# A recommender forward pass on one core: the last twenty of 80 indirect gathers issued back to back

## The chip, the cores and the metric

One NeuronCore of a Trainium2 chip runs the kernel; the other cores are idle. The metric is the device time in microseconds of one execution, and for several executions their median. The profiler records one execution; its "span" is the time from the first to the last instruction that it shows.

## The reference

A wide-and-deep model scores 2048 samples. Each sample has 13 dense numbers and eight category indices.

```python
wide = dense @ Wd_wide
for si, wi in zip(S, w):                 # eight tables of one weight per row
    wide = wide + wi[si]
wide = wide + wc0[S[3] * VOCABS[4] + S[4]]   # 140,625 rows
wide = wide + wc1[S[5] * VOCABS[6] + S[6]]   # 500,000 rows
deep_in = jnp.concatenate([dense @ Wd_deep] + [Ei[si] for Ei, si in zip(E, S)], axis=1)
h = jax.nn.relu(deep_in @ W1)            # 576 -> 512
h = jax.nn.relu(h @ W2)                  # 512 -> 256
return bias + h @ W3 + wide
```

All is float32. VOCABS is [125000, 25000, 12500, 375, 375, 1000, 500, 100], and each embedding row has 64 numbers.

## The kernel before

The 2048 samples are 16 tiles of 128, in four blocks of 512. Fields 0 to 2 have large tables, and their rows (64 embedding numbers and the wide weight, 65 in all) are fetched from HBM by indirect DMAs. The five small fields are looked up by matmuls: VectorE writes a one-hot matrix (`build_onehot`, L463) and TensorE multiplies it with the table (`look_up`, L634; `look_up_wide`, L646). The two crossed terms, `wc0` and `wc1`, are one float per sample out of large tables, and are fetched by indirect DMAs into `cross`. TensorE does layers 1 and 2 as three float32r products each (`product`, L663 to L665); ScalarE and VectorE split values into a high and a low part (L339, L343, L483, L488).

Every engine has its program written out in order, and semaphores join them.

GpSimd (POOL) issues all 80 indirect DMAs, one per tile and field, each for 128 rows. Their order is: for each of the four blocks eight gathers into `x_pair` (L289) and four into `x_two` (L297), which makes 48; then 32 gathers into `cross` (L307), c = 0 for 16 tiles and c = 1 for 16 tiles. In block 0 the 12 gathers follow one another with nothing between them. From block 1 on each gather is followed by a "pause": a memset of 128 x 320 float32 into `pause_sb`, a buffer that nobody reads (L282). Before each memset but the first, POOL waits until the one before has counted up the semaphore `paused` (L281); the memsets are all on POOL, so that wait is over when it comes. Only the very last gather, number 31 of `cross`, has no pause behind it. This document numbers the gathers of `cross` 0 to 31, as `c * TILES + t`. There are 67 pauses: 36 in blocks 1 to 3, and 31 among those of `cross`.

Each gather counts a semaphore up by 16 when its data has landed: `rows_gathered` per block for the rows, `cross_gathered[0]` and `cross_gathered[1]` for the two halves of `cross`.

The end of the kernel is on VectorE, in program order (L590 to L606): the wide sums of the gathered rows (L593, L594, L596); after a wait for all 16 gathers of c = 0 the sum with `cross[:, 0, :]` and the bias (L599); `weigh_first` and `weigh_second` of the last block (L497, L508), which TensorE's `layer3` (L720) multiplies out; the sum with the deep part (L604); and after a wait for all 16 gathers of c = 1 the last sum (L606). SyncE then stores `result` (L263).

Of the kernel before, what the change touches and what calls it, by code (L numbers as in the profile page):

```python
# [20 lines left out]
NX = len(CROSSES)  # L21
SPLIT = 3

TILES = BATCH // P
# [21 lines left out]
IDX_ROWS = NL * TILES  # L46
WARM_UP = 8
BUSY = [4, 5]


IO_ORDER = [("spread", 0, i) for i in range(NL)] + [("look", 0, i) for i in range(4)]
# [21 lines left out]
def program(nc, index, dense_t, big, small, small_w, wc, wd_rep_t, wd_wide, w1, w2, w3, bias, out):  # L73
# [6 lines left out]
    with ExitStack() as ctx:  # L80
# [185 lines left out]
        @block.gpsimd  # L266
        def _(pool):
            nc.gpsimd.memset(zero[:], 0.0).then_inc(zero_ready, 1)
            nc.gpsimd.iota(row_id[:], pattern=[[P, max(CHUNKS)]], base=0, channel_multiplier=1,
                           allow_small_or_imprecise_dtypes=True).then_inc(row_id_ready, 1)  # L270
            pool.wait_ge(zero_ready, 1)
            for m in (ident16, ident):
                nc.gpsimd.affine_select(out=m[:], in_=zero[:], compare_op=ALU.not_equal, fill=1.0, base=0,
                                        pattern=[[-1, P]], channel_multiplier=1).then_inc(ident_ready, 1)
            pool.wait_ge(ident_ready, 2)
            nc.gpsimd.memset(look_w_parts[:], 0.0).then_inc(look_w_zeroed, 1)
            nc.gpsimd.memset(ones[:], 1.0).then_inc(ones_ready, 1)
            def pause(n):

                if n:  # L280
                    pool.wait_ge(paused, n)  # L281
                nc.gpsimd.memset(pause_sb[:], 0.0).then_inc(paused, 1)  # L282

            pool.wait_ge(gather_index_ready, 1)
            pauses = 0
            for b in range(BLOCKS):
                for t in range(b * BT, (b + 1) * BT):
                    for g in (0, 1):
                        nc.gpsimd.indirect_dma_start(  # L289
                            out=x_pair[:, t, g * ROW:(g + 1) * ROW], out_offset=None, in_=big[g],  # L290
                            in_offset=bass.IndirectOffsetOnAxis(ap=idx_gather[:, g, t:t + 1], axis=0),
                        ).then_inc(rows_gathered[b][0], 16)
                        if b > 0:
                            pause(pauses)
                            pauses += 1
                for t in range(b * BT, (b + 1) * BT):
                    nc.gpsimd.indirect_dma_start(  # L297
                        out=x_two[:, t, :], out_offset=None, in_=big[2],
                        in_offset=bass.IndirectOffsetOnAxis(ap=idx_gather[:, 2, t:t + 1], axis=0),
                    ).then_inc(rows_gathered[b][1], 16)  # L300
                    if b > 0:
                        pause(pauses)
                        pauses += 1
            pool.wait_ge(cross_index_ready, 1)
            for c in range(NX):
                for t in range(TILES):
                    nc.gpsimd.indirect_dma_start(  # L307
                        out=cross[:, c, t:t + 1], out_offset=None, in_=wc[c],
                        in_offset=bass.IndirectOffsetOnAxis(ap=idx_cross[:, c, t:t + 1], axis=0),
                    ).then_inc(cross_gathered[c], 16)  # L310
                    if (c, t) != (NX - 1, TILES - 1):
                        pause(pauses)
                        pauses += 1

# [294 lines left out]
        def _(pe):  # L609
# [17 lines left out]
            def look_up(b, i):  # L627
                use = ("look", b, i)
                io_free(use)
                if b == 0 and i in (0, 2, 4):  # L630
                    pe.wait_ge(table_low, 1 + i // 2)
                for c in range(CHUNK0[i], CHUNK0[i] + CHUNKS[i]):
                    pe.wait_ge(onehot_ready, b * NCH + c + 1)
                    last = nc.tensor.matmul(io_bank(use)[:], table_hl[:, c, :], onehot[:, c, :],  # L634
                                            start=c == CHUNK0[i], stop=c == CHUNK0[i] + CHUNKS[i] - 1)
                last.then_inc(io_full, 1)
# [87 lines left out]
            def keep_busy(n):  # L724

                for _ in range(n):
                    nc.tensor.matmul(l1_ps[M1 - 1][:], zero16[:, 0:P], zero16[:], start=True, stop=True)
# [12 lines left out]
            look_up(0, 1)  # L740
            keep_busy(BUSY[0])
            pe.wait_ge(wd_loaded, 32)
            pe.wait_ge(row_index_ready, 1)
            nc.tensor.matmul(l2_ps[0:NROWS, :], wd_rep[:], w1d_sb[:], start=True, stop=True).then_inc(wdense_done, 1)
            keep_busy(BUSY[1])
            look_up(0, 2)
# [95 lines left out]
```

## Time and profile before

| | us |
|---|---|
| median of 3 runs | 136.67 |
| lowest and highest | 136.29 and 137.22 |
| the profiled execution, its own time | 137.18 |
| its span | 135.3 |

The profiled execution spent 137.18 - 135.3 = 1.9 us outside of its span. Busy time is the time in which an engine executed instructions; DMA-issuing instructions of SyncE and ScalarE are not counted as busy, but POOL's indirect DMAs are, since GpSimd works on each of them. "issue" is idle time for which the profile shows no releaser. In rows of a timeline the columns are start, duration, engine, line, operation, and in brackets how long the engine was idle before it.

### The profile page before, as it was taken

How to read it: one execution, taken by the hardware profiler on the slowest of the kernel's cores; microseconds unless marked ns; L12 is line 12 of the kernel's file. 1: busy time of each engine (PE TensorE's matmuls, PEld its weight loads, DVE VectorE, ACT ScalarE, POOL GpSimd, SP SyncE). 2: the span in 40 equal slices, each digit the busy share in tenths (PEclk: the TensorE clock that was granted, in tenths of full speed). 3: DMA queues.
4: the chain of work that ended last, by engine and by line, in shares of the span. 5: the costliest groups of instructions: out<-in, count | busy, mean ns of one | idle time of the engine just before them, and what ended most of it. 6: DMA issues, size and time to landing. Idle time of an engine off the chain costs nothing.

```text
span 135.3 us, 1728 instructions
## 1 busy us (share of the span) xinstructions
PE 112.7 (83%) x588; PEld 83.4 (62%) x588; DVE 71.7 (53%) x163; ACT 55.0 (41%) x97; POOL 110.9 (82%) x157
## 2 busy tenths in 40 slices
PE   6979999929779999999999999999999999920000
PEld 2544875726566886687888858878886788920000
DVE  2696984822399905868980166999304019310000
ACT  3698946131925224248261515456242325210000
POOL 5587877999899999989999989999998998989800
PEclk9999999995999999999999999999999999995555
DMA  4958436868632232223323320000000000000000
GB/s 138 306 115 277 29 66 28 218 122 224 207 27 22 20 26 22 20 20 20 25 19 26 22 20 0 0 0 0 5 0 0 1 0 0 5 0 0 0 3 0
DMA packets 6096, 6.90 MB, mean 51 GB/s; under 512 B 2931, under 2 KB 4115, under 8 KB 6088
## 3 DMA queue, kind: packets, MB, share of 16 engines
q0 software_dynamic: 2560, 1.62, 15.8%
q1 hardware_dynamic: 3096, 4.45, 10.8%
q10 hardware_dynamic: 432, 0.72, 1.5%
q8 instruction: 5, 0.08, 0.2%
q14 instruction: 3, 0.02, 0.1%
HBM read 6.60 MB, written 0.19 MB: 50 GB/s over the span
## 4 chain that ended last, share of the span: by engine, by line
POOL 79%; issue 11%; DMA 4%; DVE 1%; POOLq 1%; DVEq 0%
POOL x_pair L289 25%; POOL cross L307 21%; POOL pause_sb L282 21%; POOL x_two L297 12%; DMA idx_raw<-in_index_dram 2%; DMA cross<-in_wc_dram,idx_cross 2%; POOLq L80 1%; DVE idx_wrap L443 0%; DVE idx_sum L445 0%; DVE idx_look L448 0%; DVE result L606 0%; DVE idx_gather L448 0%; DVEq L605 0%
## 5 line engine op out<-in xcount | busy, mean ns | idle before, releaser
L463 DVE TENSOR_SCALAR onehot<-idx_bc,row_id 128x512 fp32r<-128x512 f16 x76 | 39.5, 586 | 4.7 <-PE io_ps L646 1.9
L289 POOL DMA_INDIRECT x_pair<-in_rows_dram,idx_gather x32 | 33.3, 1041 | 8.5 <-issue 6.2
L307 POOL DMA_INDIRECT cross<-in_wc_dram,idx_cross x32 | 30.9, 965 | 5.3 <-issue 5.3
L282 POOL MEMSET pause_sb<- 128x320 f32 x67 | 29.0, 434 | 0.0
L663 PE MATMUL l_ps<-xt_hi,w_hi 128*128 128x512 f32 x64 | 25.6, 400 | 0.0
L665 PE MATMUL l_ps<-xt_hi,w_lo 128*128 128x512 f32 x64 | 25.1, 392 | 0.0
L664 PE MATMUL l_ps<-xt_lo,w_hi 128*128 128x512 f32 x64 | 25.0, 391 | 0.0
L634 PE MATMUL io_ps<-onehot,table_hl 128*128 128x512 f32 x76 | 21.9, 414 | 0.2
L483 DVE TENSOR_TENSOR xt_lo<-io_ps,xt_hi 128x512 fp32r<-128x512 f32 (+1 forms) x8 | 5.5, 687 | 28.4 <-ACT xt_hi L339 27.5
L326 ACT CAST xt_hi<-io_ps 64x512 fp32r<-64x512 f32 x20 | 11.6, 579 | 19.8 <-PE io_ps L634 18.9
L297 POOL DMA_INDIRECT x_two<-in_rows_dram,idx_gather x16 | 16.1, 1004 | 3.2 <-issue 3.2
L634 PEld LDWEIGHTS io_ps<-onehot,table_hl 128*128 128x128 f32 x76 | 14.4, 193 | 4.4 <-DVE onehot L463 0.7
L663 PE MATMUL l_ps<-h_hi,w_hi 128*128 128x512 f32 (+1 forms) x36 | 13.4, 373 | 1.6 <-DVE h_lo L488 1.6
L352 ACT ACTIVATE h<-l_ps 128x512 f32<-128x512 f32 (+1 forms) x9 | 5.0, 551 | 22.2 <-PE l_ps L665 22.2
L663 PEld LDWEIGHTS l_ps<-xt_hi,w_hi 128*128 128x128 f32 x64 | 12.0, 188 | 2.8 <-issue 0.5
L665 PEld LDWEIGHTS l_ps<-xt_hi,w_lo 128*128 128x128 f32 x64 | 12.0, 188 | 2.6
L664 PEld LDWEIGHTS l_ps<-xt_lo,w_hi 128*128 128x128 f32 x64 | 12.0, 188 | 2.4
L665 PE MATMUL l_ps<-h_hi,w_lo 128*128 128x512 f32 (+1 forms) x36 | 13.3, 368 | 0.0
L664 PE MATMUL l_ps<-h_lo,w_hi 128*128 128x512 f32 (+1 forms) x36 | 13.2, 366 | 0.0
L488 DVE SCALAR_TENSOR_TENSOR h_lo<-l_ps,h_hi 128x512 fp32r<-128x512 f32 x16 | 10.2, 685 | 3.8 <-ACT h_hi L343 3.8
L327 ACT CAST xt_lo<-io_ps 64x512 fp32r<-64x512 f32 x20 | 11.7, 583 | 0.5
L343 ACT ACTIVATE h_hi<-l_ps 128x512 fp32r<-128x512 f32 x16 | 8.7, 600 | 3.2 <-PE l_ps L665 2.8
(75 smaller groups left out, 106.8 us busy)
## 6 DMA issues: line engine op xcount, KB each, us to landing
idx_bc<-idx_dram SPq DMA_DIRECT2D x3, 640.0 KB, 4.9
w_sb<-in_w_dram ACTq DMA_DIRECT2D x2, 256.0 KB
x_pair<-in_rows_dram,idx_gather POOLq DMA_INDIRECT x32
w_sb<-in_w_dram SPq DMA_DIRECT2D x2, 256.0 KB
w_sb<-in_w_dram SPq DMA_DIRECT2D x1, 512.0 KB
cross<-in_wc_dram,idx_cross POOLq DMA_INDIRECT x32
dense_stack<-dense_dram SPq DMA_DIRECT2D x3, 156.0 KB
table<-in_small_dram SPq DMA_DIRECT2D x1, 416.0 KB
```

Source lines behind the costliest of these rows:

```text
L282: nc.gpsimd.memset(pause_sb[:], 0.0).then_inc(paused, 1)
L289: nc.gpsimd.indirect_dma_start(out=x_pair[:, t, g * ROW:(g + 1) * ROW], out_offset=None, in_=big[g], in_offset=bass.IndirectOffsetOnAxis(a ...
L297: nc.gpsimd.indirect_dma_start(out=x_two[:, t, :], out_offset=None, in_=big[2], in_offset=bass.IndirectOffsetOnAxis(ap=idx_gather[:, 2, t: ...
L307: nc.gpsimd.indirect_dma_start(out=cross[:, c, t:t + 1], out_offset=None, in_=wc[c], in_offset=bass.IndirectOffsetOnAxis(ap=idx_cross[:, c ...
L326: nc.scalar.copy(xt_hi[b % 2][to, g, :], bank[0:D, :]).then_inc(io_act, 1)
L327: nc.scalar.copy(xt_lo[b % 2][to, g, :], bank[D:2 * D, :]).then_inc(io_act, 1)
L463: nc.vector.tensor_scalar(onehot[:, CHUNK0[i] + c, :], idx_bc[:, b, i, :], row_id[:, c:c + 1], None, ALU.is_equal).then_inc(onehot_ready, 1)
L488: nc.vector.scalar_tensor_tensor(out=h1_lo[:, m, :], in0=l1_ps[m][:], scalar=0.0, in1=h1_hi[:, m, :].bitcast(f32), op0=ALU.max, op1=ALU.su ...
L634: last = nc.tensor.matmul(io_bank(use)[:], table_hl[:, c, :], onehot[:, c, :], start=c == CHUNK0[i], stop=c == CHUNK0[i] + CHUNKS[i] - 1)
L663: nc.tensor.matmul(dst, w_hi, a_hi, start=start, stop=False)
L664: nc.tensor.matmul(dst, w_hi, a_lo, start=False, stop=False)
L665: return nc.tensor.matmul(dst, w_lo, a_hi, start=False, stop=stop)
```

## The change

A constant `DENSE_END = 20` is added, and the condition under which a gather of `cross` is followed by a pause is changed. Before, every one but number 31 was; now only numbers 0 to 11 are (32 - 20 = 12). The pauses behind numbers 12 to 30, 19 of them, are gone. The count `pauses` goes on as before, so POOL's waits for `paused` still match the memsets that remain.

```diff
 WARM_UP = 8
 BUSY = [4, 5]
+
+DENSE_END = 20
...
                         in_offset=bass.IndirectOffsetOnAxis(ap=idx_cross[:, c, t:t + 1], axis=0),
                     ).then_inc(cross_gathered[c], 16)
-                    if (c, t) != (NX - 1, TILES - 1):
+                    if c * TILES + t < NX * TILES - DENSE_END:
                         pause(pauses)
                         pauses += 1
```

## Rows read from the trace of the kernel before

**Rows 1.** The page: busy time by engine, then the chain that ended last.

```profile
PE 112.7 (83%) x588; PEld 83.4 (62%) x588; DVE 71.7 (53%) x163; ACT 55.0 (41%) x97; POOL 110.9 (82%) x157
...
POOL 79%; issue 11%; DMA 4%; DVE 1%; POOLq 1%; DVEq 0%
```

**Rows 2.** The last steps of the chain, in time: start, duration, what.

```profile
127.50 2.34 DMA cross<-in_wc_dram,idx_cross
...
129.93 0.17 DVE result L606
```

**Rows 3.** Waits of the whole run: the last sum of VectorE.

```profile
DVE result L606 <- DMA cross<-in_wc_dram,idx_cross: 9.7, 1, 9.7
```

**Rows 4.** Timeline of POOL: the gathers of cross from number 12 on.

```profile
98.69 0.95 POOL L307 DMA_INDIRECT cross<-in_wc_dram,idx_cross  x1 [0.16 <-issue]
99.65 0.38 POOL L282 MEMSET pause_sb<- 128x320 f32 x1
100.19 0.95 POOL L307 DMA_INDIRECT cross<-in_wc_dram,idx_cross  x1 [0.17 <-issue]
...
103.18 0.95 POOL L307 DMA_INDIRECT cross<-in_wc_dram,idx_cross  x1 [0.16 <-issue]
...
116.64 1.35 POOL L307 DMA_INDIRECT cross<-in_wc_dram,idx_cross  x1 [0.17 <-issue]
...
127.50 0.95 POOL L307 DMA_INDIRECT cross<-in_wc_dram,idx_cross  x1 [0.17 <-issue]
```

**Rows 5.** Timeline of POOL: gathers without pauses, block 0 and the first of block 1.

```profile
4.59 1.27 POOL L289 DMA_INDIRECT x_pair<-in_rows_dram,idx_gather  x1 [2.26 <-DVE idx_gather L448]
...
12.43 0.94 POOL L289 DMA_INDIRECT x_pair<-in_rows_dram,idx_gather  x1 [0.30 <-issue]
13.68 1.31 POOL L289 DMA_INDIRECT x_pair<-in_rows_dram,idx_gather  x1 [0.30 <-issue]
15.30 1.88 POOL L289 DMA_INDIRECT x_pair<-in_rows_dram,idx_gather  x1 [0.30 <-issue]
...
20.37 0.94 POOL L297 DMA_INDIRECT x_two<-in_rows_dram,idx_gather  x1 [0.30 <-issue]
...
23.33 0.94 POOL L289 DMA_INDIRECT x_pair<-in_rows_dram,idx_gather  x1 [0.30 <-issue]
```

**Rows 6.** Timeline of VectorE beside those gathers.

```profile
12.60 0.69 DVE L469 TENSOR_TENSOR w_lo<-w_sb,w_hi 128x512 fp32r<-128x512 f32 x1 [1.28 <-ACT w_hi L360]
...
15.39 1.67 DVE L463 TENSOR_SCALAR onehot<-idx_bc,row_id 128x512 fp32r<-128x512 f16 x4
...
20.86 0.69 DVE L483 TENSOR_TENSOR xt_lo<-io_ps,xt_hi 128x512 fp32r<-128x512 f32 x1 [0.95 <-issue]
```

**Rows 7.** Windows: each engine's busy us (x instructions), PEclk, DMA share, GB/s.

```profile
4.59:23.33 18.74, 17.52 (x100) 11.46 (x98) 14.32 (x34) 14.58 (x28) 15.08 (x12) 1.00 0.58 121
...
98.69:127.50 28.81, 20.71 (x128) 16.69 (x126) 7.40 (x15) 7.27 (x13) 25.66 (x38) 0.90 0.02 1
```

**Rows 8.** Timeline of VectorE from 98.69 us on.

```profile
102.51 0.69 DVE L483 TENSOR_TENSOR xt_lo<-io_ps,xt_hi 128x512 fp32r<-128x512 f32 x1 [6.68 <-ACT xt_hi L339]
103.12 0.79 DVE L508 SCALAR_TENSOR_TENSOR h_w<-h,w_sb,h_first 128x512 f32<-128x512 f32 x1
108.04 0.68 DVE L483 TENSOR_TENSOR xt_lo<-io_ps,xt_hi 64x512 fp32r<-64x512 f32 x1 [4.13 <-ACT xt_hi L339]
111.48 2.73 DVE L488 SCALAR_TENSOR_TENSOR h_lo<-l_ps,h_hi 128x512 fp32r<-128x512 f32 x4 [2.76 <-ACT h_hi L343]
...
114.78 0.23 DVE L599 SCALAR_TENSOR_TENSOR wide_bias<-cross,bias_sb,wide_dense 128x16 f32<-128x16 f32 x1
116.41 0.75 DVE L497 SCALAR_TENSOR_TENSOR h_first<-h,w_sb,wide_look 128x512 f32<-128x512 f32 x1 [1.40 <-issue]
117.62 0.48 DVE L508 SCALAR_TENSOR_TENSOR h_w<-h,w_sb,h_first 128x256 f32<-128x256 f32 x1 [0.46 <-ACT h L352]
118.91 0.48 DVE L508 SCALAR_TENSOR_TENSOR h_w<-h,w_sb,h_first 128x256 f32<-128x256 f32 x1 [0.80 <-ACT h L352]
120.09 0.17 DVE L604 TENSOR_TENSOR wide_deep<-wide_bias,deep_ps 128x16 f32<-128x16 f32 x1 [0.70 <-PE deep_ps L720]
```

**Rows 9.** The page: DMA issues, kind, count and median us to landing.

```profile
x_two<-in_rows_dram,idx_gather POOLq DMA_INDIRECT x16, 3.3
```

## The prediction

> **What bounds the kernel now.** I read the page's busy line first, and it alone would mislead: TensorE is busy 83% of the span and POOL 82% [rows 1]. The chain that ended last decides between them: 79% of it is POOL, 11% is POOL's own issue time, and TensorE is not in it at all [rows 1]. The end of that chain says why. The last gather of `cross` starts at 127.50 us and has landed 2.34 us later; VectorE's last sum starts at 129.93 us, and what follows it to the end of the span (135.3 - 129.93 = 5.4 us: the sum, the store and the closing of the program) hangs on nothing else [rows 2]. The waits confirm it from the other side: before that sum VectorE was idle for 9.7 us, until the gather had landed [rows 3]. So the deep part of the model had been ready for a long time: VectorE had added it in by 120.09 + 0.17 = 120.26 us [rows 8]. The kernel is a single file of 80 gathers on POOL, and whatever shortens the file by up to some 9 us shortens the kernel by as much.
>
> The timeline of POOL gives the pace of the file. With a pause one step takes 0.95 us of gather, 0.38 us of memset and 0.17 us of issue, 1.50 us in all [rows 4]. Without one (block 0) the best steps are 0.94 us of gather and 0.30 us of issue: from 12.43 to 13.68 is 1.25 us [rows 5].
>
> **What the change removes.** The pauses behind gathers 12 to 30 go, 19 of them; number 31 had none. Gather 12 still starts at 98.69 us, since all that lies before it is untouched. From there to the start of gather 31 at 127.50 us are 28.81 us for 19 steps [rows 4], 1.516 us each: 1.50 us, and once 0.40 us more, at 116.64 us, where a gather took 1.35 us.
>
> **What a step costs afterwards.** The memset's 0.38 us goes, but not all of it is won. Between a memset and the next gather POOL shows 0.17 us of issue, between two gathers 0.30 us [rows 4, 5]. So 0.13 us comes back, and a step is 0.94 + 0.30 = 1.245 us (between 1.24 and 1.25 by the rows). 19 x 1.245 = 23.66 us, if no gather is stretched. Bounds for the issue gap: it may be 0.17 us as after a memset, which would make a step 1.12 us, or 0.30 us as between two gathers. I take 0.30 us, since it is measured between exactly such a pair of instructions, eleven times in block 0 and once before the first of block 1.
>
> **Stretched gathers.** In block 0 not all steps were 1.245 us: from 4.59 to 23.33 us 12 steps took 18.74 us, 1.562 us each [rows 5, 7]. That is slower than with pauses, and it is what speaks against this change. The excess is 18.74 - 12 x 1.245 = 3.80 us. The gathers that were long lay beside VectorE's work: the one of 1.88 us at 15.30 us ran beside four one-hots that lasted 1.67 us [rows 5, 6]. VectorE was busy 14.32 us of that stretch [rows 7]. In the stretch of the change it is busy 7.40 us of 28.81 [rows 7], so I carry over a rate and not a number. Two of its kinds of work there, L483 and L488 (0.69 + 0.68 + 2.73 = 4.1 us), read one operand from PSUM and one from SBUF [rows 8]; the only one of that kind in block 0, at 20.86 us, lay beside a gather of the plain 0.94 us, the one at 20.37 us [rows 5, 6]. Without that kind the rate is 3.80 / (14.32 - 0.69) = 0.28 us of stretch for each us of VectorE, and the dense stretch has 7.40 - 4.1 = 3.3 us of it: 0.92 us. Ends: 0 us (as at 12.60 us, where a subtraction with both operands in SBUF lay inside a gather of 0.94 us, and at 103.12 us, where L508 lay beside a gather of 0.95 us) [rows 4, 5, 6, 8]; and 7.40 x 3.80 / 14.32 = 1.96 us if every kind counts. I take 0.9 us.
>
> The sum, against the profiled execution's own time: 28.81 - 23.66 - 0.9 = 4.25 us less. Gather 31 starts at 98.69 + 24.56 = 123.25 us, has landed at 125.6 us, the span ends at 135.3 - 4.25 = 131.05 us, and that execution would have taken 137.18 - 4.25 = 132.9 us. The profiled execution is 0.5 us above the median of the runs, 136.67; the saving doesn't hang on that, so the median goes to 136.67 - 4.25 = 132.4 us.
>
> **What is late next, and what hides it.** The deep part is complete at 120.26 us, 5.3 us ahead of the last landing in the forecast; it does not take over. If the issue gap were 0.17 us and nothing was stretched, the last landing would be at 98.69 + 19 x 1.12 + 2.34 = 122.3 us, still behind it. Denser gathers may also slow VectorE's work in the tail; that would have to cost over 5 us of delay before it counted. The wait for `cross_gathered[0]` ahead of L599 does not matter: gather 15 started at 103.18 us before the change [rows 4], so it had landed near 105.5 us, and VectorE came to L599 only at 114.78 us [rows 8]. The time from a gather's start to its landing could grow with more of them in flight. The rows give 2.34 us in the quiet end [rows 2] and a median of 3.3 us for gathers into `x_two` [rows 9], with rows of 260 bytes and mostly beside other transfers. DMA is 2% busy in the stretch of the change and 58% in block 0 [rows 7], so I take 2.34 us, and keep 1 us more as an end.
>
> A rule speaks against the gain. By the Trainium skill, page "SBUF — State Buffer", section "Who interferes with whom", a VectorE instruction with two SBUF inputs contends with a GpSimd instruction that reads SBUF, and whoever comes second is blocked until the other has finished. The same section infers that such an instruction leaves descriptor generation alone, since it holds only the read interface. By the first reading the sum would be that of the third rival below, by the second the saving would be the full 5.15 us. The rows lie between them: nothing at 12.60 us, something beside the one-hots.
>
> **The rivals.**
>
> *Block 0's pace returns (slightly slower).* If the stretching is not VectorE's doing but comes with gathers that follow one another, a step is 1.562 us: 19 x 1.562 = 29.68 us, 0.87 us more than now, 137.5 us. For it: the pace was measured over 12 steps. Against it: 20.37 us and 23.33 us show plain gathers of 0.94 us inside the same unbroken run, and DMA traffic and VectorE were both far busier there. Chance 0.03.
>
> *The gathers back up (slower).* POOL may only be so many gathers ahead of the landing; once that room is used up, each gather waits for a landing, and a step becomes 2.34 us. The 12 gathers of block 0 and the first of block 1 went without such a wait, so it decides from the thirteenth gather of an unbroken run on. The new run has 20, so 8 steps are longer by 2.34 - 1.245 = 1.1 us each, 8.8 us, against 4.25 us saved: 4.5 us more, 141.2 us. For it: no unbroken run of that length is in the trace. Against it: at a step of 1.25 us and 2.34 us to landing only two are in flight at a time. Chance 0.02.
>
> *VectorE shuts POOL out (less gain).* Each instruction of VectorE with both large operands in SBUF holds up the gather beside it for its whole length: 0.79 + 0.75 + 0.48 + 0.48 = 2.50 us [rows 8]. Then 28.81 - 23.66 - 2.50 = 2.65 us are saved, 134.0 us. For it: the gather at 116.64 us, beside L497 at 116.41 us, was 0.40 us longer [rows 4, 8]. Against it: that is half of L497's length, and at 103.12 us nothing was lost. Chance 0.12.
>
> *The issue gap shrinks to 0.17 us (more gain).* 28.81 - 19 x 1.12 - 0.9 = 6.6 us, 130.0 us. For it: the stretch has idle engines all around. Against it: 0.30 us came out the same in each of the twelve cases. Chance 0.03.
>
> That the change does nothing has little room: the memsets are on POOL's own chain and the chain is the end. Something that I have not seen gets 0.01 of no change.
>
> **How the numbers follow.** My forecast, 132.4 us, gets 0.79; its own spread comes from the stretch (0 to 1.96 us: 131.5 to 133.5 us) and from the landing (up to 1 us more). The range takes in the rival at 134.0 us as its upper end, and goes below 131.5 us by 0.3 us for the scatter of the medians: 131.2 to 134.0 us. A difference of about 1%, 1.4 us, is what a measurement of this kernel can tell from none. Faster by more: the forecast, the shut-out and the shrunken gap, 0.79 + 0.12 + 0.03 = 0.94. Within it: block 0's pace and the unseen, 0.04. Slower: the backing up, 0.02.
>
> **What would show it.** In the changed kernel's timeline of POOL, 48 memsets of `pause_sb` instead of 67; gather 12 of `cross` near 98.7 us; between the gathers behind it 0.30 us of issue and no memset; most of them 0.94 to 0.95 us long, and a few longer ones, all beside VectorE's L497 and L508. VectorE's wait ahead of L606 should be 9.7 - 4.25 = 5.4 us and still end with the gather. The prediction is wrong if the gathers beside L488 are stretched, if the gap is not 0.30 us, if gathers from the thirteenth on take longer than those before, if the last one takes much more than 2.34 us to land, or if L604 ends later than 125 us.

## The result, and the profile after

The changed kernel took 145.22 us (median of 4 runs, 143.91 to 145.59) beside 136.84 us before: a ratio of 1.060, with an interval of 1.052 to 1.068. It is slower by 8.4 us where 132.4 us was forecast. The profiled execution took 143.91 us, its span is 142.1 us.

The page of the changed kernel (its line numbers are 2 higher), busy time and the chain that ended last:

```profile
PE 121.0 (85%) x588; PEld 86.7 (61%) x588; DVE 71.6 (50%) x163; ACT 54.9 (39%) x97; POOL 102.1 (72%) x138
...
PE 69%; another core or an unknown queue 13%; issue 7%; ACT 5%; DVE 2%; ACTq 1%; DVEq 0%
```

Against [rows 1] POOL is gone from the chain and TensorE is in it. But POOL did exactly what was forecast. Its timeline, the last pause, the gathers 12 to 14 and the last:

```profile
96.04 0.55 POOL L284 MEMSET pause_sb<- 128x320 f32 x1
96.75 1.03 POOL L309 DMA_INDIRECT cross<-in_wc_dram,idx_cross  x1 [0.16 <-issue]
98.09 1.19 POOL L309 DMA_INDIRECT cross<-in_wc_dram,idx_cross  x1 [0.30 <-issue]
99.58 0.94 POOL L309 DMA_INDIRECT cross<-in_wc_dram,idx_cross  x1 [0.30 <-issue]
...
121.31 0.94 POOL L309 DMA_INDIRECT cross<-in_wc_dram,idx_cross  x1 [0.30 <-issue]
```

From gather 12 to gather 31 are 121.31 - 96.75 = 24.56 us, the number of the forecast to the digit (in part by luck, see below); before it was 28.81 us [rows 4]. Gather 12 started 1.9 us earlier than before, since the twelve dense gathers of block 0 went faster in this execution. POOL was done at 122.25 us. The time was lost elsewhere. The waits of the changed kernel:

```profile
DVE xt_lo L485 <- ACT xt_hi L341: 40.2, 7, 18.7
ACT wide_look L336 <- remote: 24.2, 2, 19.0
...
DVE onehot L465 <- remote: 6.4, 1, 6.4
```

"remote" (on the page "another core or an unknown queue") stands for a wait whose release the trace does not hold. Only one core runs here, so it isn't another core. The longest such wait is ScalarE's, for the copy of the last block's wide look-up. The timelines of TensorE and of ScalarE around it:

```profile
107.61 1.32 PE L648 MATMUL io_ps<-onehot,look_w_parts 128*32 128x512 bf16 x19
...
111.83 0.27 PE L661 MATMUL io_ps<-ident,x_two 128*65 128x128 f32 x1 [0.34 <-issue]
...
116.81 0.58 PE L665 MATMUL l_ps<-xt_hi,w_hi 128*128 128x512 f32 x1 [0.86 <-issue]
...
122.47 0.59 PE L667 MATMUL l_ps<-xt_hi,w_lo 128*128 128x512 f32 x1 [1.52 <-issue]
127.14 0.80 PE L665 MATMUL l_ps<-xt_hi,w_hi 128*128 128x512 f32 x1 [4.08 <-DVE xt_lo L485]
```

```profile
105.73 0.59 ACT L341 CAST xt_hi<-io_ps 128x512 fp32r<-128x512 f32 x1
125.31 0.59 ACT L336 COPY wide_look<-io_ps 128x512 f32<-128x512 f32 x1 [18.98 <-remote]
125.79 0.58 ACT L341 CAST xt_hi<-io_ps 64x512 fp32r<-64x512 f32 x1
```

TensorE finished the 19 matmuls at 107.61 + 1.32 = 108.93 us. A signal is here the semaphore update by which TensorE tells other engines that a matmul is done. The copy waits for that of the last of the 19, and for `h2_used` of block 1, which is long past. It starts at 125.31 us: the signal came 16.4 us late. The transposes of `x_two` end at 112.10 us, and their copy starts right behind the first one, so both signals were there once the gathers had ended. In between TensorE itself hardly moves: from 112.53 to 122.47 us it starts 12 matmuls that need nothing but TensorE's own queue, many of them 0.7 to 2.1 us apart.

The rest is passed on. VectorE's L485 of that block starts at 126.40 us where it started at 108.04 us before [rows 8], 18.4 us later. The idle time then costs 1.4 us more. Its sequel, from there to L606, takes 139.88 - 126.40 = 13.5 us instead of 12.05 us, with the granted clock at 1.2 GHz for the first twelve matmuls behind the gap (0.50 of full speed from 118 to 132.4 us), 0.43 us apart instead of 0.23 us. So the last sum waits for the deep part now: L606 (L604 before) starts at 139.88 us. The last sum starts at 140.09 us, 10.2 us later than before, and the close behind it takes 2.0 us, not 5.4 us (more on that at the end): 10.2 - 3.4 = 6.8 us, the difference of the spans. Some 4 us of the 18.4 us were lost earlier, in block 0, whose twelve gathers always were dense: there ScalarE's first wide copy came at 28.19 us, for matmuls that had ended at 22.99 us; in the trace of the kernel before it came at 24.03 us.

### The profile page after: what moved, and what is told of

The parts are those of the page before. It is cut to its first block, busy times and chain, and to the rows that moved or that the text cites. A ratio compares the mean times of both kernels' runs of the same rounds, so it can differ in the third digit from the quotient of the medians.

```text
span 142.1 us, 1709 instructions
## 1 busy us (share of the span) xinstructions
PE 121.0 (85%) x588; PEld 86.7 (61%) x588; DVE 71.6 (50%) x163; ACT 54.9 (39%) x97; POOL 102.1 (72%) x138
## 3 DMA queue, kind: packets, MB, share of 16 engines
q0 software_dynamic: 2560, 1.62, 16.3%
## 4 chain that ended last, share of the span: by engine, by line
PE 69%; another core or an unknown queue 13%; issue 7%; ACT 5%; DVE 2%; ACTq 1%; DVEq 0%
PE l_ps L665 16%; PE l_ps L667 15%; PE l_ps L666 15%; PE io_ps L636 12%; PE io_ps L648 3%; PE io_ps L661 2%; PE l_ps L695 2%; PE l_ps L729 1%; DVE onehot L465 1%; PE deep_ps L722 1%; ACT idx_bc L321 1%; ACT L358 1%; ACT xt_hi L341 1%; PE l_ps L746 1%
## 5 line engine op out<-in xcount | busy, mean ns | idle before, releaser
L291 POOL DMA_INDIRECT x_pair<-in_rows_dram,idx_gather x32 | 32.0, 1000 | 8.4 <-issue 6.2
L665 PE MATMUL l_ps<-xt_hi,w_hi 128*128 128x512 f32 x64 | 27.4, 428 | 5.7 <-DVE xt_lo L485 4.1
L667 PE MATMUL l_ps<-xt_hi,w_lo 128*128 128x512 f32 x64 | 26.7, 418 | 3.0 <-issue 2.9
L666 PE MATMUL l_ps<-xt_lo,w_hi 128*128 128x512 f32 x64 | 26.5, 414 | 0.3 <-issue 0.3
L485 DVE TENSOR_TENSOR xt_lo<-io_ps,xt_hi 128x512 fp32r<-128x512 f32 (+1 forms) x8 | 5.5, 687 | 41.8 <-ACT xt_hi L341 40.2
L284 POOL MEMSET pause_sb<- 128x320 f32 x48 | 21.4, 445 | 0.0
L665 PEld LDWEIGHTS l_ps<-xt_hi,w_hi 128*128 128x128 f32 x64 | 12.8, 199 | 11.1 <-DVE xt_lo L485 5.1
L665 PE MATMUL l_ps<-h_hi,w_hi 128*128 128x512 f32 (+1 forms) x36 | 14.2, 394 | 3.2 <-issue 3.2
L667 PEld LDWEIGHTS l_ps<-xt_hi,w_lo 128*128 128x128 f32 x64 | 12.8, 200 | 6.0 <-issue 3.3
L666 PEld LDWEIGHTS l_ps<-xt_lo,w_hi 128*128 128x128 f32 x64 | 12.9, 201 | 4.4 <-issue 2.0
L336 ACT COPY wide_look<-io_ps 128x512 f32<-128x512 f32 x4 | 2.3, 586 | 30.2 <-remote 24.2
L490 DVE SCALAR_TENSOR_TENSOR h_lo<-l_ps,h_hi 128x512 fp32r<-128x512 f32 x16 | 10.2, 684 | 5.1 <-ACT h_hi L345 5.1
```

Of the source, the lines that this page charges most:

```text
L291: nc.gpsimd.indirect_dma_start(out=x_pair[:, t, g * ROW:(g + 1) * ROW], out_offset=None, in_=big[g], in_offset=bass.IndirectOffsetOnAxis(a ...
L490: nc.vector.scalar_tensor_tensor(out=h1_lo[:, m, :], in0=l1_ps[m][:], scalar=0.0, in1=h1_hi[:, m, :].bitcast(f32), op0=ALU.max, op1=ALU.su ...
L665: nc.tensor.matmul(dst, w_hi, a_hi, start=start, stop=False)
L666: nc.tensor.matmul(dst, w_hi, a_lo, start=False, stop=False)
L667: return nc.tensor.matmul(dst, w_lo, a_hi, start=False, stop=stop)
```

## The experiments

The versions ran in six groups, each group within minutes on one chip, beside runs of the kernel before. Of the edits only the lines that matter are shown. Some versions leave work out: the short look-up 15 of the 19 table chunks of the last block, the version without gathers the last twenty gathers, the versions with half the rows 64 rows of each of them. Where gathers or rows are left out, `cross` is zeroed beforehand. Theory A was that TensorE's signals are held up when its burst of short matmuls (the wide look-up) falls into the dense run. Theory B was the length or pace of the dense run, whatever TensorE does. Theory C was a condition of the chip or of the time, which the dense gathers only let show.

**1 to 4 (first group): where the dense run stands, the burst, a break, no gathers.**

```diff
-DENSE_END = 20
+DENSE_END = 12
```

> Only the last twelve gathers follow one another without a pause; the run then starts near 110 us, when TensorE has its wide look-up of the last block (19 short matmuls) behind it. Theory A (TensorE's semaphore updates are held back only if its burst of short matmuls falls into the dense run): no stall, 11 pauses less at 0.25 us each, 136.8 - 2.8 = 134 us. Theory B (it is the length of the dense run: after some ten gathers at a step of 1.25 us something is full, whatever TensorE does): a stall only from about 122 us on, when the deep part is done, so also about 134 us, or slower if it comes sooner. Theory C (any dense run beside TensorE's full stream holds it back): over 137 us.

```diff
-                for c in range(NCH):
+                for c in (range(NCH) if b < BLOCKS - 1 else range(groups)):
...
-                                            start=c < groups, stop=c >= NCH - groups)
+                                            start=c < groups, stop=c >= (NCH if b < BLOCKS - 1 else groups) - groups)
```

> The changed kernel with its twenty dense gathers; the wide look-up of the last block is cut from 19 matmuls to 4 (15 of its 19 table chunks are left out). Theory A: without the burst no stall, the gathers decide and the time is 132 to 133 us. Theory B: ScalarE still waits long for its copy of the wide look-up or for the value after it, 140 us and more.

```diff
+                    elif c * TILES + t < NX * TILES - 1:
+                        pause(pauses, 1)
+                        pauses += 1
```

> The changed kernel, but each of the last gathers is again followed by a memset, of one column in place of 320 (about 0.10 us): the step is 0.95 + 0.10 + 0.17 = 1.22 us, as without a pause. If the pace of the gathers does it, the stall is there and the time 142 to 146 us. If a break by another instruction is enough, whatever its length, there is no stall and the time is near 131 to 132 us.

```diff
+                    if c * TILES + t >= NX * TILES - DENSE_END:
+                        for _ in range(2):
+                            pool.wait_ge(paused, pauses)
+                            nc.gpsimd.memset(pause_sb[:].bitcast(bf16), 0.0).then_inc(paused, 1)
+                            pauses += 1
+                        continue
...
-            dve.wait_ge(cross_gathered[1], 16 * TILES)
+            dve.wait_ge(paused, 36 + NX * TILES - DENSE_END + 2 * DENSE_END)
```

> The last twenty gathers are left out (that part of the crossed terms is zero) and POOL is kept busy by two memsets of 0.63 us in the place of each, a step of about 1.27 us. If gathers are what holds TensorE back, no stall: POOL ends near 98.7 + 20 x 1.27 = 124 us and the deep part at 120 to 124 us, total about 130 to 132 us. If the stall has nothing to do with the gathers' own work, it stays.

Measured beside 137.69 us of the kernel before: 134.70 us with twelve dense gathers (ratio 0.978, 0.973 to 0.982), and in one run each 132.2 us with the short look-up, 131.93 us with the narrow memsets and 134.95 us without gathers. The last is above the 130 to 132 us expected because the two memsets took 1.38 us and not 1.27 us. No trace of the four has a "remote" wait. It looked like theory A, and like a break being enough. Neither follows, because the changed kernel had not been run in that group.

**5 and 6 (second group): the changed kernel again, and the narrow memset timed.**

> The changed kernel itself, unaltered, on a chip beside runs of the kernel before. The runs with a narrow memset and with a short look-up had no stall, but neither has been compared with the changed kernel on one chip. If the dense run and the burst do it, the changed kernel is at 143 to 146 us here too, with ScalarE waiting some 19 us for its copy of the wide look-up. Theory C (the stall belongs to a condition of the chip or of the recording under which the first comparison ran, and the dense gathers only let it show): no stall here, 132 to 133 us, about 0.965 of before.

> The twenty last gathers, each followed by a memset of one column, timed beside the changed kernel: 131.9 us again. Theory A and the theory of the pace leave it without a stall only if the break itself matters; theory C has it equal to the changed kernel within 0.5%.

The changed kernel took 144.07 us beside 137.92 us (1.048, 1.040 to 1.056). The narrow memset, 131.93 us in the first group, took 138.14, 144.05, 144.57 and 144.28 us here. In three of four runs a break in the run didn't help, and the group matters. The trace is of the run of 138.14 us. TensorE's last matmul of layer 1, then ScalarE's four copies, one for each bank of layer 1:

```profile
110.79 0.39 PE L670 MATMUL l_ps<-xt_hi,w_lo 128*128 128x512 f32 x1
```

```profile
113.28 0.60 ACT L348 ACTIVATE h_hi<-l_ps 128x512 fp32r<-128x512 f32 x1 [5.89 <-remote]
116.14 0.60 ACT L348 ACTIVATE h_hi<-l_ps 128x512 fp32r<-128x512 f32 x1 [2.25 <-remote]
121.07 0.60 ACT L348 ACTIVATE h_hi<-l_ps 128x512 fp32r<-128x512 f32 x1 [4.33 <-remote]
125.33 0.60 ACT L348 ACTIVATE h_hi<-l_ps 128x512 fp32r<-128x512 f32 x1 [3.67 <-remote]
```

All four banks were done by 111.18 us. Their signals came one at a time, all before the last gather of the dense run ended (124.49 + 0.95 = 125.44 us). So the signals are not shut out for the length of the run; they get through slowly.

From then on a version is only read beside a sign of which condition its group was in.

**7 to 10 (third group): the changed kernel, and three of the four versions beside it.**

> The changed kernel beside the three that follow, all on one chip, since the narrow memset took 131.9 us on one chip and 138 to 144 us on another, and the changed kernel was never on the first. If the stall depends on the chip, this reads either 132 to 133 us or 143 to 146 us; the others are to be read against it.

> The wide look-up of the last block cut from 19 matmuls to 4 (15 of 19 table chunks left out). Beside a changed kernel that stalls: under theory A 132 to 133 us; if the pace of the gathers alone does it, beside any full stream of TensorE, 140 us and more. Beside one that doesn't stall: no information.

> The last twenty gathers left out, memsets of 2 x 0.63 us in the place of each. Beside a changed kernel that stalls: if gathers load what TensorE's signals need, 134.9 us and no stall; if it is anything about POOL being busy, a stall and 140 us and more.

> The last twelve gathers dense. Beside a changed kernel that stalls: theory A gives 134 to 135 us with no wait of ScalarE over 4 us; if a dense run anywhere in TensorE's last 10 us of work is enough, TensorE ends later than 120 us and the time is over 137 us.

Beside 136.66 us: the changed kernel 143.63 us (1.049, 1.029 to 1.068), the short look-up 134.48 and 138.43 us, no gathers 134.42 us, twelve dense gathers 134.34 us (0.981, 0.967 to 0.995).

The trace of the changed kernel shows whose signals are late. ScalarE:

```profile
103.20 0.58 ACT L336 COPY wide_look<-io_ps 128x512 f32<-128x512 f32 x1 [3.49 <-PE io_ps L648]
111.03 0.58 ACT L341 CAST xt_hi<-io_ps 64x512 fp32r<-64x512 f32 x1 [7.25 <-remote]
127.17 2.06 ACT L345 ACTIVATE h_hi<-l_ps 128x512 fp32r<-128x512 f32 x4 [15.56 <-remote]
```

TensorE, VectorE and POOL of the same trace:

```profile
104.02 0.60 PE L661 MATMUL io_ps<-ident,x_two 128*65 128x128 f32 x4
...
112.38 0.80 PE L665 MATMUL l_ps<-xt_hi,w_hi 128*128 128x512 f32 x1 [5.01 <-issue]
...
117.24 0.45 PE L667 MATMUL l_ps<-xt_hi,w_lo 128*128 128x512 f32 x1
```

```profile
111.64 0.68 DVE L485 TENSOR_TENSOR xt_lo<-io_ps,xt_hi 64x512 fp32r<-64x512 f32 x1 [10.55 <-issue]
127.80 2.48 DVE L490 SCALAR_TENSOR_TENSOR h_lo<-l_ps,h_hi 128x512 fp32r<-128x512 f32 x4 [15.48 <-ACT h_hi L345]
```

```profile
122.66 0.94 POOL L309 DMA_INDIRECT cross<-in_wc_dram,idx_cross  x1 [0.30 <-issue]
```

ScalarE's copy ends at 111.61 us and VectorE starts at 111.64; VectorE ends at 112.32 and TensorE starts at 112.38. Those signals take 0.03 and 0.06 us. TensorE's own are late: the transposes end at 104.62 us and ScalarE starts 6.4 us later; the first bank of layer 1 is done 3 matmuls behind 112.38 us, at 114.03 us, and ScalarE starts at 127.17 us, 13 us later and 3.6 us after the last gather's end. The lateness grows along the dense run and ends some 3 us behind its last gather. TensorE meanwhile does its 12 matmuls at their usual spacing for 1.2 GHz (0.43 us) and then has nothing left that it may do.

The short look-up refutes theory A as it was put. Without the burst the signals were late as well, only later:

```profile
106.98 2.64 ACT L345 ACTIVATE h_hi<-l_ps 128x512 fp32r<-128x512 f32 x4 [2.86 <-PE l_ps L667]
116.23 0.60 ACT L354 ACTIVATE h<-l_ps 128x512 f32<-128x512 f32 x1 [6.61 <-remote]
127.48 0.66 ACT L354 ACTIVATE h<-l_ps 128x256 f32<-128x256 f32 x2 [10.66 <-remote]
```

By 110 us TensorE's signals were still in time, and the four copies of layer 1 were through. The last two signals of layer 2, for matmuls that ended near 113 and 114.6 us, came together at 127.48 us. The burst may still add to the lateness: with it the first late signal was that of the transposes that ended at 104.62 us. How much it adds was not measured.

Without gathers at the end nothing was late there, in the same group. Its only "remote" waits lie in block 0, where the gathers stayed dense:

```profile
DVE onehot L474 <- remote: 4.6, 1, 4.6
...
ACT wide_look L345 <- remote: 2.2, 1, 2.2
```

So at the end it is the gathers, and not POOL being busy; which part of a gather does it (its descriptors, its transfers or its sixteen semaphore updates) no version separates. With twelve dense gathers the signals were late too, but the deep part had 5 us in hand, and it ended at 121.45 us, ahead of the last landing:

```profile
117.73 0.38 ACT L354 ACTIVATE h<-l_ps 128x256 f32<-128x256 f32 x1 [3.28 <-remote]
```

```profile
121.28 0.17 DVE L606 TENSOR_TENSOR wide_deep<-wide_bias,deep_ps 128x16 f32<-128x16 f32 x1 [2.65 <-remote]
```

**11 to 14 (fourth group): the control, two paces, half the rows.** The pause of 160 columns is the edit of the narrow memset with 160 in place of 1.

> The changed kernel as the control of its chip for the three that follow: 143 to 146 us, with waits of ScalarE of 14 us and more for a signal of TensorE, if this chip is like three of the four seen so far.

> Each of the last nineteen steps has a memset of 160 columns (about 0.22 us): the step is 0.95 + 0.22 + 0.17 = 1.34 us, halfway between 1.25 and 1.50. If TensorE's signals fall behind in proportion to how far the pace is above what is bearable, the delay is smaller than the changed kernel's by about half: 137 to 141 us. If there is a sharp bound between 1.34 and 1.50 us per step it is 142 to 146 us; if it is between 1.25 and 1.34 us, no stall and 136.8 - 19 x 0.16 = 134 us.

```diff
+                    rows = P if c * TILES + t < NX * TILES - DENSE_END else P // 2
-                        out=cross[:, c, t:t + 1], out_offset=None, in_=wc[c],
+                        out=cross[0:rows, c, t:t + 1], out_offset=None, in_=wc[c],
...
-                    if c * TILES + t < NX * TILES - DENSE_END:
+                    if c * TILES + t < NX * TILES - 1:
                         pause(pauses)
```

> The last twenty gathers fetch 64 rows in place of 128 (the other half of these crossed terms is left at zero), and each is followed by the full memset. If GpSimd's time of a gather is mostly per row, a step is about 1.1 us, so that more gathers but fewer rows come in a microsecond than in the changed kernel. If the rows (descriptors and their packets) are what the signals of TensorE queue behind: no stall, and 136.8 - 19 x 0.4 = 129 us. If it is the number of gathers, each with its sixteen semaphore updates: a stall and over 138 us.

```diff
-DENSE_END = 20
+DENSE_END = 12
...
-                nc.gpsimd.memset(pause_sb[:], 0.0).then_inc(paused, 1)
+                nc.gpsimd.memset(pause_sb[:, 0:240], 0.0).then_inc(paused, 1)
```

> A version that may beat both: the last twelve gathers dense as before, and all other pauses 240 columns long (0.30 us in place of 0.38), a step of 1.42 us. 56 pauses save 0.08 us each, 4.5 us, on top of 2.8: 129.5 us if the signals of TensorE stay in time, and POOL's last gather lands near 119 us, about with the deep part. If 1.42 us is already too fast, TensorE falls behind over the whole second half and the time is over 137 us.

Beside 137.05 us the unaltered changed kernel took 132.90 and 132.97 us: a ratio of 0.969 (0.961 to 0.976). That is the forecast, and not the 143 to 146 us expected by then. Its timelines of POOL and of VectorE:

```profile
99.07 0.95 POOL L309 DMA_INDIRECT cross<-in_wc_dram,idx_cross  x1 [0.17 <-issue]
100.33 1.37 POOL L309 DMA_INDIRECT cross<-in_wc_dram,idx_cross  x1 [0.30 <-issue]
102.00 0.94 POOL L309 DMA_INDIRECT cross<-in_wc_dram,idx_cross  x1 [0.30 <-issue]
...
123.23 0.94 POOL L309 DMA_INDIRECT cross<-in_wc_dram,idx_cross  x1 [0.30 <-issue]
```

```profile
117.10 0.17 DVE L606 TENSOR_TENSOR wide_deep<-wide_bias,deep_ps 128x16 f32<-128x16 f32 x1 [0.70 <-PE deep_ps L722]
125.81 0.17 DVE L608 TENSOR_TENSOR result<-wide_deep,cross 128x16 f32<-128x16 f32 x1 [8.54 <-DMA cross<-in_wc_dram,idx_cross]
```

The nineteen steps take 24.16 us, one gather is stretched by 0.43 us, the last sum waits for the gather for 8.5 us, and no wait is "remote". The same program is worth -4 us or +6 to +8 us, by a condition that the kernel does not set. The other three say little about the late signals in such a group: 133.30 and 135.54 us with 160 columns, 137.20 us with half the rows and full pauses, 132.13 us with pauses of 240 columns (0.963, 0.957 to 0.969; 129.5 us was expected). Half the rows did not make a gather much shorter, 0.90 to 0.91 us instead of 0.95, so that expectation of a step of 1.1 us failed (it was 1.45 us), and the time was that of the kernel before.

**15 to 18 (fifth and sixth group): the two open questions, once without and once with late signals.** In half_dense the last twenty gathers have 64 rows and no pauses.

> All pauses but the last 240 columns long, the last twelve gathers dense: 132.1 us on a chip on which the changed kernel had no stall. On a chip of the other kind, where TensorE's signals come late in a dense run: if 1.42 us a step is borne, again 132 to 133 us, with a delay only in the last twelve steps; if not, lateness grows over blocks 1 to 3 and the time is over 137 us.

> The last twenty gathers without pauses and with 64 rows each in place of 128 (the other half of these crossed terms is left at zero): a step of about 0.91 + 0.30 = 1.21 us, so as many gathers and as many semaphore updates as in the changed kernel, and half the rows. On a chip of the kind with late signals: 144 us if the number of gathers does it, 132 to 133 us if their rows do. On the other kind of chip 132 us, and no information.

> As the two runs before, once more, since both fell on chips without late signals: 132 us there. On a chip with late signals 132 to 133 us if 1.42 us a step is borne, over 137 us if not.

> As before, once more, for the other kind of chip: 144 us if the number of gathers loads TensorE's signals, 132 to 133 us if their rows do; 132 us and no information on a chip without late signals.

In the fifth group both took 132 us (132.09 and 132.32 beside 137.40). The sixth came on the same chip, number 10, and there half the rows took 144.27 and 144.15 us beside 137.25 us (1.052, 1.046 to 1.058), and the pauses of 240 columns took 144.74, 145.48, 132.27 and 136.80 us. ScalarE and POOL in the trace with half the rows:

```profile
102.95 0.59 ACT L345 CAST xt_hi<-io_ps 128x512 fp32r<-128x512 f32 x1
122.49 0.58 ACT L340 COPY wide_look<-io_ps 128x512 f32<-128x512 f32 x1 [18.95 <-issue]
126.83 0.58 ACT L345 CAST xt_hi<-io_ps 64x512 fp32r<-64x512 f32 x1 [3.75 <-remote]
```

```profile
120.45 0.90 POOL L313 DMA_INDIRECT cross<-in_wc_dram,idx_cross  x1 [0.30 <-issue]
121.65 0.90 POOL L313 DMA_INDIRECT cross<-in_wc_dram,idx_cross  x1 [0.31 <-issue]
```

Two things follow. The condition isn't a trait of the chip, since chip 10 had both. And halving the rows doesn't help, since 20 gathers of 64 rows hold TensorE's signals for as long as 20 of 128: the wide copy starts 16.3 us behind its matmuls, which ended at 106.15 us (16.4 us in the first trace). From 128 to 64 rows the lateness goes with the number of gathers in a time, and not with the rows. Theories B and C both hold in part: the dense gathers are needed, and so is a condition that changes with time.

Whether a step of 1.42 us is already too fast is not decided. That version has twelve dense gathers at the end as well, and twelve in block 0 like every version. Its trace (the run of 144.74 us) has late signals long behind block 0's dense run, whose last gather ends at 25.11 us. TensorE's second look-up for block 1 and ScalarE's copy of it:

```profile
35.30 0.96 PE L636 MATMUL io_ps<-onehot,table_hl 128*128 128x512 f32 x3 [2.50 <-issue]
```

```profile
41.97 0.58 ACT L328 CAST xt_hi<-io_ps 64x512 fp32r<-64x512 f32 x1 [6.11 <-remote]
```

But so has the first trace of the changed kernel, in the same place, with full pauses and a step of 1.50 us:

```profile
33.45 0.97 PE L636 MATMUL io_ps<-onehot,table_hl 128*128 128x512 f32 x3
```

```profile
36.41 0.58 ACT L328 CAST xt_hi<-io_ps 64x512 fp32r<-64x512 f32 x1 [2.72 <-remote]
```

The signal is 5.7 us late with the short pauses and 2.0 us late with the full ones. ScalarE's four wide copies, one per block, start 3.72, 1.03, 0.05 and 4.86 us behind the end of their matmuls with the short pauses, and 5.20, 0.73, 0.05 and 16.38 us with the full ones. So behind block 0 the lateness dies away at either step. But with the short pauses TensorE has lost more by then: L510 of block 2 starts at 113.60 us, in the fourth group at 100.81 us, and the dense run at the end meets more of its work. One run of four, 132.27 us, had no loss.

## Why the prediction was wrong

*What bounds the kernel, and the pace.* Right. The chain was POOL's, a step without a pause is 1.245 us with 0.30 us of issue, the run of nineteen steps took 24.56 us in the first trace and 24.16 us in the control, against 24.56 us forecast. 48 memsets were left. That the first trace hit 24.56 us to the digit is luck: three of the four large instructions that the 0.9 us was reckoned for (L499 and both L510 of the last block) ran only at 136 to 139 us, behind the dense run, and the gathers that took longer were those at 96.75, 98.09 and 107.07 us.

*Stretched gathers.* 0.9 us was taken; it was 24.56 - 23.66 = 0.9 us in the first trace and 0.5 us in the control. The shut-out rival (2.5 us) did not happen: the longest hold was 0.51 us, of the gather at 107.07 us beside an L510 of 0.74 us. But the mechanism behind it is there. VectorE and POOL, in the first trace:

```profile
106.96 0.74 DVE L510 SCALAR_TENSOR_TENSOR h_w<-h,w_sb,h_first 128x512 f32<-128x512 f32 x1
```

```profile
107.07 1.45 POOL L309 DMA_INDIRECT cross<-in_wc_dram,idx_cross  x1 [0.30 <-issue]
```

The gather ends 0.82 us after L510 does. The gather at 100.33 us in the control ends 0.83 us behind an L510 (100.13 us, 0.74 us long), and the gather at 116.64 us in the kernel before 0.83 us behind L497 [rows 4, 8]. The three gathers of the control that began before an L499 or L510 were not stretched at all, and the one at 103.18 us in the kernel before, which began only 0.06 us behind L508, was not either. So a gather is held until such an instruction is over, but only if it starts while that instruction is well under way, and then only for what is left of it. My rival charged the full length of every one. The rule from the Trainium skill that goes with it (page "SBUF — State Buffer", section "Who interferes with whom": a VectorE instruction with two SBUF inputs contends with a GpSimd instruction that reads SBUF, and whoever comes second is blocked) fits these three rows. The second reading, by which such an instruction leaves gathers alone, does not.

*Landing.* 2.34 us was taken; the control shows 2.48 us.

*What is late next.* This step failed. I took the deep part as fixed at 120.26 us, with 5.3 us in hand, and thought only of VectorE being slowed by dense gathers. In the runs it was TensorE whose completion signals came late in the dense run, by 16.4 us in the first trace, and L606 started at 139.88 us, 19.8 us later than before ("L604 ends later than 125 us" was the sign of being wrong that came true). The rival that gathers back up had the wrong party waiting: POOL never waited, from the first dense gather to the last, while it was ScalarE that waited for TensorE.

*What could have been seen.* The trace of the kernel before has twelve dense gathers in block 0 and no late signal there (ScalarE's wide copy at 24.03 us after 0.74 us of idle time), so it gave no row for this. What was in reach was the question: I asked what the dense run does to POOL's own pace and to VectorE, and not what it does to the signals that other engines wait for, although the run covered all of TensorE's last 20 us of work. Nothing in that trace told that they would be late. The chance of 0.94 for a gain rested on one trace of one execution.

*The amount.* The changed kernel was measured four times, the first time and in groups 2, 3 and 4. In three of them, with late signals, it cost 4.8 to 6.0%; in the one without it gained 3.1%. So the sum of the forecast, 4.25 us, is confirmed as the gain on POOL's path (137.05 - 132.94 = 4.1 us), and in the other condition it is lost to new waits, the longest of them 14.3 to 19.0 us in the three traces.

A version that is better than the kernel before in either condition is the one with twelve dense gathers: 134.70 us without late signals (0.978) and 134.34 us with them (0.981). Its dense run begins near 110 us, so that the little that TensorE still has to signal is covered by the slack. Without late signals the changed kernel gains more (0.969), but only there. The pauses of 240 columns are faster in one condition (132.1 us) and not safe in the other.

What remains open: why a group has one condition or the other, and what the signals queue behind. The records themselves suffer too. The control's trace holds 2331 semaphore updates, and those of the first, fourth and fifth group 2319 to 2351 (2046 without the gathers). Those of groups 2, 3 and 6 and the first trace of the changed kernel hold 1461 to 1774. The trace of the kernel before, taken with that first trace, holds 1928 and shows no late signal. So records are lost wherever signals are late, and in one trace where none is. All runs were taken with the profiler's record of their spans, so whether the signals are late in an execution that nobody records, or the recording itself is what delays them, was not tried. Nor was the half of it tried that lies in TensorE, its rate of matmuls: in three traces (the first one, the second group's and the sixth group's with half the rows) TensorE's own matmuls also stood apart while its signals were late.

## What to carry to other kernels

A pause that looks like waste on the chain that ends last may be what lets the other engines go on in time: before taking it out, ask which engines still have signals to send while the faster stream runs, and move the dense part behind the last of them. Slack in the other path is a cover only if the change can't touch that path. And a version that wins once is compared with the original change on the same chip at the same time, and then once more at another time, before it is believed; here the first four experiments alone would have led to a wrong cause.

## What the runs showed of the hardware that was not expected

- In three of six groups and in the first measurement TensorE's completion signals reached their waiters late while indirect DMAs of GpSimd followed one another at 1.21 to 1.25 us a step: by 16.4 us in the first trace, by 18.6 us in the second group's (transposes ended at 108.59 us, ScalarE's copy at 127.18 us). They came one at a time. ScalarE's and VectorE's signals took 0.03 and 0.06 us in the same stretch, and in the third group the last of twelve dense gathers still landed within 2.45 us. At 1.50 us the kernel before showed no loss in any group (136.3 to 138.3 us in all its runs but one, which took 139.3 us in the sixth group), but its deep part has 9.7 us in hand, so that a small lateness would not show.
- A gather of 64 rows of 4 bytes costs GpSimd 0.90 us and one of 128 rows 0.95 us, and twenty of either delay TensorE's signals alike (144.2 and 143.6 to 145.2 us).
- A gather of 128 rows that starts at least 0.1 us into a VectorE instruction with two SBUF inputs ends 0.82 or 0.83 us after that instruction (the three traces above); in the control those that start before it take their plain 0.94 to 0.95 us.
- The close of the program goes with how TensorE stood at the end. Waits of SyncE's queue, first in the control of the fourth group, where TensorE had been idle for some 9 us when the result was stored:

```profile
SPq L82 <- PEq L82: 3.4, 1, 3.4
```

and in the first trace of the changed kernel, where TensorE's last matmul ended just before the last sums:

```profile
SPq L82 <- PEq L82: 0.2, 1, 0.2
```

It is 3.5 us in the kernel before. In the other traces it is 0.2 us in the six where TensorE had just finished, and 3.3 to 3.7 us in the eleven where it had been idle for 5 us or more before the last sum. So 3.3 us of the loss on the deep part were given back behind the last sum; why, no run tells.
